# Routing a mixture of experts batch by batch inside the attention stage, into fixed regions per expert, and summing the results by accumulating gathers

## What is computed

```python
x = x + _L1_xattn_ref(_layernorm(x), ctx_512, ctx_512)        # 32 query heads, 8 key heads of 16
def _routed_moe(x, gate_w, w0, w1, wo):                       # x = layernorm of all 2048 tokens
    logits = jnp.einsum('td,de->te', x, gate_w)               # 8 experts
    top_logits, top_idx = jax.lax.top_k(logits, K)            # K = 2
    top_w = jax.nn.softmax(top_logits, axis=-1)
    cw = jnp.zeros((T, E)).at[jnp.arange(T)[:, None], top_idx].add(top_w)
    for e in range(E):
        h = jax.nn.silu(x @ w0[e]) * (x @ w1[e])              # w0, w1: 512 x 1024
        out = out + cw[:, e:e + 1] * (h @ wo[e])              # wo: 1024 x 512
    return out
x = x + _routed_moe(_layernorm(x), ...)
```

## Time and profile before

| | |
|---|---|
| time, median of 3 runs | 2035.28 us (2032.77 to 2039.09) |
| time of the profiled execution | 2037.96 us |
| its span, first to last instruction | 2036.1 us |
| PE, DVE, ACT, POOL busy | 79%, 48%, 35%, 33% |
| Hadamard matrix loaded, `phase_b` begins | 214.7 us |
| context loaded again, `phase_b` ends | 693.9 us |
| last unit's `add_attended` | 1154.65 us |
| first matmul of expert tile 0 | 1268.21 us |
| store of the last expert tile landed | 1983.67 us |

### The profile page before, as it was taken

One profiled execution on the slowest core, in us unless ns is written; L12 is line 12 of the kernel. 1 busy time (PEld: TensorE's weight loads), 2 busy tenths in 40 slices (PEclk: granted clock), 3 DMA queues, 4 the chain that ended last, 5 costly groups with the idle time before them and its releaser, 6 DMA issues.

```text
span 2036.1 us, 25086 instructions
## 1 busy us (share of the span) xinstructions
PE 1600.3 (79%) x7951; PEld 1063.5 (52%) x7952; DVE 980.0 (48%) x1543; ACT 703.3 (35%) x1117; POOL 673.8 (33%) x428
## 2 busy tenths in 40 slices
PE   4333578788877549999998761999999999999980
PEld 2222345354545324333333360787878888788870
DVE  2788565656556358888888420222221222222214
ACT  2343344353534217777776510111111111111110
POOL 1322051423314313131314225466276152720006
PEclk7666689899989759999999855999999999999995
DMA  7020000000000044444542036144043040420007
GB/s 281 1 83 0 21 1 0 0 0 0 0 0 0 21 109 124 131 140 139 168 144 68 4 132 238 39 150 155 31 155 144 31 155 31 155 103 31 31 21 247
DMA packets 74989, 166.98 MB, mean 82 GB/s; under 512 B 6834, under 2 KB 8371, under 8 KB 74291
## 3 DMA queue, kind: packets, MB, share of 16 engines
q1 hardware_dynamic: 58578, 129.01, 18.9%
q10 hardware_dynamic: 11232, 20.45, 2.9%
q0 software_dynamic: 5120, 16.78, 2.5%
HBM read 112.74 MB, written 52.95 MB: 81 GB/s over the span
## 4 chain that ended last, share of the span: by engine, by line
PE 58%; issue 14%; DVE 10%; POOL 9%; DMA 4%; ACT 3%; SPq 1%; POOLq 0%; DVEq 0%; ACTq 0%
PE psum L1595 9%; PE psum L1597 9%; PE psum L1596 9%; PE psum L1403 6%; DVE neg_max L1089 5%; PE psum L1429 4%; PE psum L1513 4%; PE psum L1502 3%; PE psum L1475 3%; POOL expert_weight_parts L682 3%; PE psum L1439 2%; PE psum L1366 2%; DMA w_of_even_expert<-in_L_ffn_w 1%; POOL normed_all L672 1%; PE psum L1619 1%
## 5 line engine op out<-in xcount | busy, mean ns | idle before, releaser
L1089 DVE TENSOR_REDUCE neg_max<-psum 128x2 f32<-128x1024 f32 x256 | 300.3, 1220 | 79.4 <-PE psum L1475 79.1
L849 ACT ACTIVATE probabilities<-psum 128x512 f32<-128x512 f32 x512 | 272.1, 600 | 86.5 <-PE psum L1502 81.5
L1595 PE MATMUL psum<-expert_weight_parts,sorted_tokens_t_first 128*128 x624 | 250.6, 402 | 10.6 <-POOL expert_weight_parts L682 7.5
L1597 PE MATMUL psum<-expert_weight_parts,sorted_tokens_t_second 128*128 x624 | 246.1, 394 | 0.0
L1596 PE MATMUL psum<-expert_weight_parts,sorted_tokens_t_first 128*128 x624 | 245.8, 394 | 0.0
L1206 DVE TENSOR_TENSOR expert_inner<-psum,expert_inner 128x512 f32<-128x512 f32 x78 | 53.9, 692 | 386.8 <-ACT expert_inner L885 386.8
L1475 PE MATMUL psum<-key_rows,query_rows 48*128 48x512 f32 x512 | 165.1, 502 | 29.5 <-DMA query_rows<-query_rows_of_units 18.4
L885 ACT ACTIVATE expert_inner<-psum 128x512 f32<-128x512 f32 x78 | 46.6, 598 | 396.9 <-PE psum L1597 396.9
L1502 PE MATMUL psum<-query_rows,key_rows 50*128 50x512 f32 x512 | 177.1, 443 | 6.8 <-ACT probabilities L849 3.7
L1513 PE MATMUL psum<-probabilities,value_and_one 128*32 128x512 f32 x1024 | 140.3, 621 | 0.0
L1595 PEld LDWEIGHTS psum<-expert_weight_parts,sorted_tokens_t_first 128*128 128x128 f32 x624 | 119.0, 191 | 36.9 <-issue 12.4
(11 more groups left out here) (225 smaller groups left out, 2874.7 us busy)
## 6 DMA issues: line engine op xcount, KB each, us to landing
w_of_odd_expert<-in_L_ffn_w SPq DMA_DIRECT2D x8, 2048.0 KB, 9.3
wo_of_expert<-in_L_ffn_wo SPq DMA_DIRECT2D x7, 2048.0 KB, 8.6
query_rows<-query_rows_of_units SPq DMA_DIRECT2D x64, 192.0 KB, 4.3
w_of_even_expert<-in_L_ffn_w SPq DMA_DIRECT2D x6, 2048.0 KB, 12.0
sorted_x<-zero_rows SPq DMA_DIRECT2D x13, 768.0 KB, 4.5
sorted_tokens<-sorted_x ACTq DMA_DIRECT2D x39, 256.0 KB, 2.7
sorted_y<-expert_out ACTq DMA_DIRECT2D x39, 256.0 KB, 2.1
query_rows_of_units<-dims_first SPq DMA_DIRECT2D x32, 256.0 KB
```

The costliest lines, as they stand in the source:

```text
L849: nc.scalar.activation(prob[t % 2][:, i * SEQ:(i + 1) * SEQ], bank[4 + n % 3], ACT.Exp, scale=HD ** -0.5).then_inc(c_e, 1)
L1089: nc.vector.tensor_reduce(of_pair[:, p, st, :], ring(("max", (m, i))).rearrange("p (h n) -> p h n", h=2), AX.X, ALU.max, negate=True).then ...
L1595: nc.tensor.matmul(out_bank, hi[:, cols], w_r[:, bass.ds(w_at, 512)], start=start, stop=False)
L1597: return nc.tensor.matmul(out_bank, lo[:, cols], w_r[:, bass.ds(w_at, 512)], start=False, stop=stop)
```

## The change

1. **Fixed regions.** `sorted_x` has 2048 rows for each expert (and 7 x 128 at the end), 17280 rows instead of 4992. A token's row no longer depends on the other experts' counts, so a batch can be placed as soon as its own logits and the counts of earlier batches are known. SP writes zeros to all of it in nine pieces, and to the rows of `sorted_y` that lie beyond the 32 full tiles, during `phase_b`.
2. **Routing inside attention.** Batches 0, 1 and 2 are routed in units 11 to 16, 19 to 24 and 26 to 31: POOL normalises four tiles (`batch_rows`), ACT copies them (`copy_rows`), PE transposes them and does the `logits` and `rank` matmuls in the two places of the ring, ACT reads those out, DVE does `choose` (one part in each step of the unit), `row_weights` and `slots`, and POOL scatters eight times (`scatter`). Only batch 3 is left for `phase_d`. X is saved to `out` by batch. The halves of the first expert are split in units 27 to 30.
3. **Rows carry their weight.** A row of `sorted_x` has 528 numbers, the last 16 hold the softmax weight; DVE copies it from the loaded tile (`row_weight`), and the move of the result out of PSUM multiplies by it.
4. **Accumulating gathers.** `plan` has five columns: where a tile's rows begin in its region, and where its result goes. The results of tiles without tokens go behind the others. POOL waits for the stores of the tiles with tokens alone (`all_i["stored"]`), then gathers 16 tiles with an add into `X2`, waits for all, gathers the other 16 with an add, and SP stores each.

```diff
-ROWS = MTILES * P
+REGION = TILES * P
+ROWS = EXPERTS * REGION + (EXPERTS - 1) * P
+WIDE = D + 16
...
+        ROUTED_AT = {0: 11, 1: 19, 2: 26}
+        for b_, u_ in ROUTED_AT.items():
+            routing_jobs[(u_ + 1, 3)] = [("xt", (b_, 0))]
+            routing_jobs[(u_ + 2, 1)] = [("xt", (b_, 1))]
+            routing_jobs[(u_ + 2, 3)] = [("logits", b_)]
+            routing_jobs[(u_ + 4, 1)] = [("rank", b_)]
...
+            sp.wait_ge(d_zero, 1)
+            n = ROWS // P // ZEROED
+            for piece in range(ZEROED):
+                sp.dma_start(sorted_x[at:at + size * P, :].rearrange("(t p) c -> p t c", p=P),
+                             zero_rows[:].rearrange("p (t c) -> p t c", t=1).broadcast_to([P, size, WIDE])).then_inc(d_zf, 16)
             sp.wait_ge(b_x, BATCH * ST)
...
-                    if u in (26, 27, 28, 29):
-                        if u % 2 == 0:
+                    if routing(u, 0) is not None:
+                        batch_rows(routing(u, 0))
+                    if routing(u, 5) is not None:
+                        scatter(routing(u, 5))
+                    if u in (27, 28, 29, 30):
+                        i, h = (u - 27) // 2, (u - 27) % 2
+                        if h == 0:
                             w_in_ready(0)
-                        half_split(w_in_raw[0][(u - 26) // 2], W_IN[0][(u - 26) // 2], u % 2, w_in_parts, u % 2)
+                        half_split(w_in_raw[0][i], W_IN[0][i], h, w_in_parts, h)
+            def scatter(b):
+                for st in range(ST):
+                    t = b * ST + st
+                    for k in range(2):
+                        pool.indirect_dma_start(out=sorted_x, out_offset=bass.IndirectOffsetOnAxis(ap=slot[k][:, t:t + 1], axis=0),
+                                                in_=xr[b][k][:, st * WIDE:(st + 1) * WIDE], in_offset=None).then_inc(d_sc[b % 2], 16)
...
             def phase_d():
                 pool.wait_ge(c_x, UNITS)
-                pool.wait_ge(c_var, 2)
-                nc.gpsimd.tensor_tensor(rstd_all[:], ve_all[:], half_neg_all[:], ALU.pow).then_inc(c_rstd, 1)
-                pool.wait_ge(d_xn, TILES)
+                inverse_deviation(BATCH - 1)
+                scatter(BATCH - 1)
+                pool.wait_ge(*scattered(2))
                 wo_split(0)
...
+                pool.wait_ge(x_back, 16)
+                for parity in range(2):
+                    stored_of = pool.value_load(all_i["stored"][0:1, parity:parity + 1], min_val=1, max_val=16 * MTILES)
+                    pool.wait_ge(e_st[parity], stored_of)
+                for k in range(2):
+                    for t in range(TILES):
+                        pool.indirect_dma_start(out=X2[:, t * D:(t + 1) * D], out_offset=None, in_=sorted_y[0:MTILES * P, :],
+                                                in_offset=bass.IndirectOffsetOnAxis(ap=slot_y[k][:, t:t + 1], axis=0),
+                                                compute_op=ALU.add).then_inc(got, 16)
+                    if k == 0:
+                        pool.wait_ge(first_got, 16 * TILES)
...
+                    if routing(u, 1) is not None:
+                        copy_rows(routing(u, 1), t)
+                    if t == 3 and routing(u, 1) is not None:
+                        batch_transposed(routing(u, 1), 0)
+                    if t == 1 and routing(u, 2) is not None:
+                        batch_transposed(routing(u, 2), 1)
...
+                    if routing(u, 3) is not None:
+                        choose(routing(u, 3), t)
+                    if t == 1 and routing(u, 4) is not None:
+                        row_weights(routing(u, 4))
+                    if t == 2 and routing(u, 4) is not None:
+                        slots(routing(u, 4))
...
+                def row_weight(i, parity):
+                    dve.wait_ge(e_ld[parity], 8 * (i - parity) + 16)
+                    nc.vector.tensor_copy(row_w[parity][:], x_in[parity][:, D:D + 1]).then_inc(e_xw, 1)
...
-                nc.vector.tensor_copy(y_out[parity][:], bank[7]).then_inc(e_y, 1)
+                nc.vector.tensor_scalar(y_out[parity][:], bank[7], row_w[parity][:, 0:1], None, ALU.mult).then_inc(e_y, 1)
```

516 lines of the change are left out of this document (339 added, 177 removed).

## The result

| kernel | median, us | runs, us | ratio to before, 95% interval |
|---|---|---|---|
| before | 2034.03 | 2030.99 to 2039.09 (4) | |
| changed | 1999.87 | 1997.15 to 2002.55 (4) | 0.9829 [0.9806, 0.9853] |

What follows compares the result with a forecast made beforehand. PE was taken to set the pace in attention and the expert loop, with serial chains at head and tail. From 2037.96 us, tail -52, head -66, attention +25, less 2.7 gave 1942 us; range for 8 in 10, 1920 to 1976.

Steps and rivals of the forecast that it cites:

- The tail: After the last tile's store: the 32 gathers and additions go, hidden beside tiles without tokens; -52 us.
- limit of 2.1: In the tail: the accumulating gathers fit in the free 77.7 us if each costs less than 2.1 us.
- between about 1865 and 1930: Sign of being right: the stretch, in us, in which the accumulating gathers would run.
- The head: Last addition to first expert matmul: 43.6 us instead of 112.8, last addition 3.3 later; -66 us.
- The zeros: SP's fill in phase_b: 36.5 MB, 209 us at 175 GB/s within 479; no cost, slower-than-before rival 0.02.
- The attention: Routing of three batches beside PE's work in the attention units: +25 us, bounds 12 and 55.
- that is 7.5 a batch: Attention: PE's and ACT's units +1.7 and +2.9, DVE's choose +0.9, row_weights and slots +2; 22.5 for three batches.
- the rival with 0.15: Attention pays twice as much, with the clock's fall after waits: +55 instead of +25, 1972 us; chance 0.15.
- The port's net of +1: Attention, DVE beside POOL's weight splits: units 27 and 28 as before, 29 some 4 more, 30 meets no cast; about +1.
- the signs: Signs of being right: last tile's store ends the chain, head 44 to 50 us with 8 scatters, routed units 1 to 4 longer.
- signs of being wrong: PE's clock below 0.9 in units 12 to 25, gathers past the last tile, DVE's small operations above 1 us, late zeros.
- The loop: Expert tiles, first expert matmul to last tile's result: 17.73 us a tile, all PE; change forecast 0.

Runs made afterwards that it cites:

- e6: Changed kernel with the two sorted_tokens_t parts at a multiple of 2048 bytes in their SBUF region and row weights last; 1997.3 us, ratio 0.9829.
- e13: e10 with the logits a step earlier, so that DVE's choice stands where the changed kernel has it; 1946.5 us, ratio 0.9579.
- e1: Changed kernel with POOL's normalisation of a routed batch behind the chunk's split and ahead of the next addition; 1988.9 us, ratio 0.9777.
- e11: Changed kernel with POOL's four first-expert weight splits moved from units 27 to 30 to units 27, 28, 31 and the head; 1987.8 us, ratio 0.9753.
- e5: Changed kernel with the gathers waiting for the last tile's store instead of the last tile with tokens; 2070.4 us, ratio 1.0186.
- e8: Changed kernel with the edits of e1, e6 and e11, DVE's slots spread, scatters spread, logits in four groups; 1964.8 us, ratio 0.9674.
- e2: Changed kernel with three of four blocks of each logit left out, 4 matmuls a batch instead of 16; 1986.4 us, ratio 0.9778.
- e12: e8 with a batch's 16 logits matmuls in one row and DVE's choice a step earlier; 1958.9 us, ratio 0.9610.
- e14: e12 with an unread matmul of 48 rows and 512 columns added behind each tile's four logits matmuls; 1971.4 us, ratio 0.9702.
- e10: e8 with logits from four matmuls of 512 moving tokens, router weights held, then one 128x8 matmul per tile; 1956.3 us, ratio 0.9591.
- e7: Changed kernel with a batch's 16 logits matmuls in four groups over four steps and DVE's choice a step later; 2001.1 us, ratio 0.9845.

## Why the prediction missed

**The tail** was right, in place and size: -51.0 for -52, gathers of 1.85 us under the limit of 2.1. They ran from 1920 to 1991 and not "between about 1865 and 1930", later by the attention's excess.

**The head** was right in its steps, and 4 us short: 47.7 for 43.6. Of these 2.5 are the logits. The earlier trace rows counts two records for a matmul; the text took 0.21 us as the price of one and wrote "sixteen logits matmuls 3.4", where 32 records were to be paid: 5.9 measured. The last addition came 3.1 us later for 3.3, by batch 2's scatters ahead of it.

**The zeros** cost next to nothing, as said: pieces of 4 MB landed in 31.6 us, the last was issued at 295 us, and the context's load behind them went out 1.5 us later than before.

**The attention** is the step that failed: "that is 7.5 a batch ... together +23.5 ... +25", for which +73.2 was measured. Three things were wrong in it.
- The clock was left out of the sum. Waits were to cost their own length, and half-speed time was counted only beside POOL's splits and in the rival with 0.15, at six units of 5 us. The changed kernel has 88.7 us more of it, worth up to 44 of the 73 us (up to 36 in e6, whose attention is the same code). e13 has 20.5 us at half speed and an attention of 285.5 for 331.2 us: 24 more than before the change, near the 25 of the forecast. It is not quite the work that was forecast: its logits cost PE half of those in the changed kernel, and two of POOL's splits and batch 2's scatters stand elsewhere. So the sum was of the right order for a kernel in which the clock stays up; that each of its terms was right is not shown.
- POOL's and SP's queues were not followed for the moved normalisation. The text gave batch_rows no place in the sum; it stood 8.25 us ahead of the split, for which SP waits, with PE's rows behind it (e1: 5.5 us in each of two units).
- The port's net of +1 supposed that "units 27 and 28 as before", 29 some 4 longer and 30 untouched. The choice and the slots met the splits in 29 and 30, and 5 to 12 us depend on it (e11 against e5 and the changed kernel).

The prices on PE and DVE were low as well: 16 logits are 4.1 us at full clock (e8: 12.5 for 48), not 1.9, and DVE had 15.6 us of work in unit 15, 5.5 more than in a plain unit, where 3.3 were expected.

Of the signs, the chain's end, the 44 to 50 us of the head and its eight scatters came as said. "Units 12, 13, 15 and their likes 1 to 4 us longer" did not: they are 7.1, 8.8 and 5.4 longer, and the longest is 13, not 29. Two of the signs of being wrong appeared: a clock below 0.9 in units 12 and 13 (0.84 and 0.74), and small operations of DVE above 1 us.

**The loop** was put at no change and is 4.4 us longer: 0.25 us a tile by the place of two tiles in SBUF (e6), less the time by which PE now waits less for POOL.

The rival "attention pays twice as much" named the right cause, the clock's fall after a wait, and +55 for the +73.2 measured; its 1972 lay near the range's upper end of 1976, and the result is 28 us above it. What stays open: why PE stands in units 17 and 25 of the changed kernel, and what exactly lets the clock fall. It followed waits of 1.2 to 3.8 us and rows of short matmuls, but e2, e8, e12 and e14 show that where it does not fall in one unit, it may in the next.

## What to carry to other kernels

Where PE sets the pace with nothing to spare, work put beside it is not paid by its length but by what PE does meanwhile: count behind each wait that it causes (1.2 to 3.8 us here) a stretch at half speed (3 to 10 us in most cases here, 31 in the changed kernel's worst, and none in some), and look first at which instructions of other queues stand behind each one that is moved in. Place such work by trial in small parts: e13 and e10 do the same work in places one step apart, and their attentions differ by 10 us.
When the same code runs twice, its slow stretches need not be the same ones (e5 and e6): read an edit from the units it touches, and from others that it leaves alone as well.
Price a form of instruction by the records of its row and the number that the code issues, both.

## What the runs showed of the hardware

- TensorE's granted clock fell from 1.00 to 0.50 while PE was busy without a gap, in a row of 16 matmuls of 8 columns (938 to 942 us), and stayed there with full-size matmuls until 946. Before that it had been 1.00 since 930, with one gap of 0.2 us on PE.
- Matmuls of 512 columns whose held operand began 128 bytes past a multiple of 2048 bytes of the region took 0.232 us from start to start, 0.227 at the multiple: 0.25 us a tile, back to 17.7 us in e6. The matmuls on `expert_inner_t` took 0.229 and 0.228.
- An accumulating gather of 128 rows of 2 KB costs POOL 1.54 us (1.85 with its gap) and lands 5.5 to 9.4 us after its issue; a scatter costs POOL 0.96 (1.27).
- Beside these gathers, with the DMA engines busy throughout (1.06 from 1960 to 1978), PE worked without a gap; one tile of 18 us was 0.5 us longer.
- A DVE operation of 0.19 us with two inputs in SBUF took 1.57, 2.41 and, in e7, 4.41 us beside POOL's cast and subtraction of 128x2048; a reduction beside the same cast took its 0.19.
- Four matmuls with 32 columns held and 512 moving, each into its own 32 rows, take 1.04 us together at full clock (e10), no more than four of 128x8 (1.03 to 1.06 in e8).
